# Start of a fused attention and expert kernel: first rows of three weights spread by TensorE, weights of pairs 0 and 1 prepared first, first projections in two bank pairs

## The chip, the cores and the metric

One core of one Trainium2 chip runs the whole program. The time is device microseconds of one execution. Three executions of the kernel before stand beside one profiled execution. Engines: PE is TensorE, DVE is VectorE, ACT is ScalarE, POOL is GpSimd, SP is SyncE. Each works through its own list of instructions in order, and semaphores tie the lists together.

## The reference

```python
x = states                                    # (4, 1024, 128) f32
n = layernorm(x)
q, k, v = (tanh(n @ W + b) for W, b in ((Wq, bq), (Wk, bk), (Wv, bv)))   # 16 heads of 64
a = softmax(causal(q @ k.T / sqrt(64)));  y = tanh((a @ v) @ Wo + bo)
x = x + layernorm(y)
# a second, latent attention (16 heads of 4), a router over 8 experts, top 2, 256 wide
x = x + layernorm(latent_attention_and_experts(layernorm(x)))
```

## The kernel before

The work is 4 batches of 1024 rows times 8 pairs of heads, so 32 pairs. A pair has five groups of score matmuls (`scores`), each read by an exponential on ACT (`exp`), masked at the diagonal on POOL (`mask`), summed on DVE and multiplied with the values on PE (`context`). While pair i runs, values, queries and keys of pair i + 1 are projected (`values`, `project`) and go through tanh on ACT. After the 32 pairs the latent attention and the experts follow.

Matmuls of f32 accuracy are made of f16 halves: a high part (ACT) and the remainder, the low part (DVE). The states are kept turned, with a first column of ones in place of a feature. So that this column carries the bias, the bias takes the place of row 0 of each weight, and row 0 of the weight is subtracted from every other row (`less_first`, L292). For Wv and Wq, PE spreads row 0 over the partitions by a matmul of a row of ones with it into PSUM (L331, banks 2-3 and 4-5). For Wk the row arrives spread by two broadcasting DMAs (L238). `less_first` and `weights_lo` work on all 8 pairs of heads of one weight at a time, 128x1024.

The program starts with a block of its own (L228). In it SP issues, in this order, the load of batch 0, two first rows, the spread Wk row, three bias rows, small weights, eight tiny pieces of latent biases, the other three batches and Wo (`@block.sync`). ACT issues the loads of Wv, Wq, Wk and four biases. DVE takes the moments of batch 0, normalises it and makes the weights, PE turns the batch (`turn_normal`), ACT and DVE split it (`states_hi`, `states_lo`). The block ends with a barrier of all five engines: nothing of the second block runs before the last of them, SP too, has issued its last instruction of the first.

The second block (L2397) starts on PE with `values(0)`, then `project(0, 0)` (queries) and `project(0, 1)` (keys), all three through the same two PSUM banks 4 and 5 (PJ), so that each waits for the tanh that empties them; then `scores(0, 0)`. DVE takes moments of batches 1 to 3 and normalises them meanwhile; POOL makes their deviations by two instructions (`state_deviation`, L195 and L197). PE turns batch 1 and 2 in pair 0 and batch 3 in pair 1, as each pair up to 1 has a free place in PJ. Pairs 0 to 3 are written out, then a loop follows. Within a pair PE's order is fixed by `pair` in `first_tensor`: `context(i, 3)` waits for the second mask of the pair, and the turning of the next batch stands behind it.

Of the kernel before, what the change touches and what calls it, by code (L numbers as in the profile page):

```python
# [82 lines left out]
def build(nc, states, Wq, bq, Wk, bk, Wv, bv, Wo, bo, q_w, q_b, k_w, k_b, v_w, v_b, o_w, o_b,  # L83
# [7 lines left out]
    with ExitStack() as ctx:  # L91
# [66 lines left out]
        a0 = Arena(a1.at)  # L158
        w_in = a0.take(3 * H1 * DH).rearrange("p (t n) -> p t n", t=3)
        wo_in0 = hs[:, 3 * T:3 * T + PAIRS, :]  # L160
        w_first = a0.take(3 * H1 * DH).rearrange("p (t n) -> p t n", t=3)
# [4 lines left out]
        small_in, w_got, first_got = sem("small_in"), sem("w_got"), sem("first_got")  # L166
        first_clear, w_less = sem("first_clear"), sem("w_less")
# [3 lines left out]
        SPREAD = {2: bank(2, 2), 0: bank(4, 2)}  # L171
# [55 lines left out]

        with nc.Block() as block:  # L228
            @block.sync
            def _(sp):  # L230
# [4 lines left out]
                for t, w in ((2, Wv), (0, Wq)):  # L235
                    sp.dma_start(first_rows[0:1, t, :], w[0:1, :]).then_inc(rows_got, 16)
                for rows in REST:
                    sp.dma_start(w_first[rows, 1, :], Wk[0, :].partition_broadcast(rows.stop - rows.start)  # L238
                                 ).then_inc(first_got, 16)
                for t, bias in ((2, bv), (0, bq), (1, bk)):  # L240
                    sp.dma_start(w_in[0:1, t, :], bias.rearrange("(a n) -> a n", a=1)).then_inc(first_got, 16)
# [16 lines left out]
            def _(act):  # L258
                for t, w in ((2, Wv), (0, Wq), (1, Wk)):
                    for rows in REST:  # L260
                        act.dma_start(w_in[rows, t, :], w[rows, :]).then_inc(w_got, 16)
# [3 lines left out]
                for k, (t, slot) in enumerate(((2, VSLOT), (0, QSLOT), (1, KSLOT))):  # L265
                    act.wait_ge(w_less, k + 1)
                    nc.scalar.activation(W_all[:, :, slot, :], w_in[:, t, :].rearrange("p (n c) -> p n c", n=PAIRS),
                                         ACT.Copy, scale=WSCALE).then_inc(whi_done, 1)
# [3 lines left out]
            def _(pool):  # L272
                nc.gpsimd.memset(w_first[0:1, 1, :], 0.0).then_inc(first_clear, 1)
# [17 lines left out]
            def _(dve):  # L291
                def less_first(k):  # L292
                    t = (2, 0, 1)[k]
                    if k == 0:
                        dve.wait_ge(first_clear, 1)
                        dve.wait_ge(w_got, 16 * 6)
                        dve.wait_ge(first_got, 16 * 5)
                    if t in SPREAD:
                        dve.wait_ge(first_spread, k + 1)
# [2139 lines left out]
```

## Time and profile before

| what | us |
|---|---|
| three executions | 1686.24, 1686.81, 1693.86 (median 1686.81) |
| the profiled execution | 1692.87 |
| its span | 1690.9 |
| PE busy | 1620.2 (96% of the span) |
| DVE, ACT, POOL busy | 1437.7, 1207.2, 456.0 |
| chain that ended last | PE 86%, DVE 6%, ACT 3%, issue 2%, POOL 1% |

The profile lists busy time per engine and the chain of work that ended last, followed back from the end through whatever released each step. PE is the engine of that chain nearly throughout. The start is another matter: the first two of forty slices of the span show PE 4 tenths busy and then 9 tenths.

### The profile page before, as it was taken

How to read it: one execution, taken by the hardware profiler on the slowest of the kernel's cores; microseconds unless marked ns; L12 is line 12 of the kernel's file. 1: busy time of each engine (PE TensorE's matmuls, PEld its weight loads, DVE VectorE, ACT ScalarE, POOL GpSimd, SP SyncE). 2: the span in 40 equal slices, each digit the busy share in tenths (PEclk: the TensorE clock that was granted, in tenths of full speed). 3: DMA queues.
4: the chain of work that ended last, by engine and by line, in shares of the span. 5: the costliest groups of instructions: out<-in, count | busy, mean ns of one | idle time of the engine just before them, and what ended most of it. 6: DMA issues, size and time to landing. Idle time of an engine off the chain costs nothing.

```text
span 1690.9 us, 38163 instructions
## 1 busy us (share of the span) xinstructions
PE 1620.2 (96%) x14822; PEld 713.5 (42%) x14822; DVE 1437.7 (85%) x2093; ACT 1207.2 (71%) x1205; POOL 456.0 (27%) x564
## 2 busy tenths in 40 slices
PE   4999999999999999998999999999999999989996
PEld 2444444444444444445233333333332332466774
DVE  6677778888888888897999999999999999478888
ACT  2776666666667666654887888788878888656776
POOL 2311112332322333332234232323332331220004
PEclk9999999999999999998999999999999999989998
DMA  5311101111011001011012000200030000000001
GB/s 153 71 37 38 37 20 39 38 37 37 36 37 37 34 24 38 22 32 32 14 39 49 11 13 16 48 14 13 17 73 22 14 16 14 1 1 14 13 12 50
DMA packets 46754, 53.39 MB, mean 32 GB/s; under 512 B 9309, under 2 KB 33581, under 8 KB 46638
## 3 DMA queue, kind: packets, MB, share of 16 engines
q1 hardware_dynamic: 45588, 50.06, 10.3%
q10 hardware_dynamic: 1050, 1.73, 0.4%
q8 instruction: 80, 1.31, 0.3%
q14 instruction: 36, 0.29, 0.1%
HBM read 15.59 MB, written 10.49 MB: 15 GB/s over the span
## 4 chain that ended last, share of the span: by engine, by line
PE 86%; DVE 6%; ACT 3%; issue 2%; POOL 1%; ACTq 0%; POOLq 0%; DVEq 0%
PE psum L1807 15%; PE psum L567 15%; PE psum L548 11%; PE psum L1792 9%; PE psum L1818 7%; PE psum L512 5%; PE psum L1448 5%; PE psum L1413 4%; PE psum L585 3%; DVE arena L2268 3%; PE psum L605 2%; PE psum L530 1%; ACT arena L2036 1%; PE psum L532 1%; PE psum L531 1%
## 5 line engine op out<-in xcount | busy, mean ns | idle before, releaser
L2268 DVE TENSOR_REDUCE arena<-psum 128x2 f32<-128x1024 f32 x490 | 585.6, 1220 | 39.0 <-PE psum L1818 33.0
L2036 ACT ACTIVATE arena<-psum 128x1024 f32<-128x1024 f32 x512 | 523.8, 1025 | 132.0 <-PE psum L1792 118.0
L721 ACT ACTIVATE arena<-psum 128x2048 f32<-128x2048 f32 (+1 forms) x160 | 274.0, 1712 | 231.6 <-PE psum L548 231.4
L1807 PE MATMUL psum<-arena 128*32 128x256 f32 x4096 | 327.9, 392 | 0.7
L813 POOL TENSOR_SCALAR_AFFINE_SELECT arena<-arena 128x512 f32<-128x512 f32 (+1 forms) x160 | 151.7, 966 | 521.9 <-ACT arena L721 521.9
L567 PE MATMUL psum<-arena,hs 128*64 128x512 f32 (+3 forms) x1536 | 283.0, 496 | 0.1
L548 PE MATMUL psum<-arena 64*128 64x512 f16 (+3 forms) x2304 | 216.3, 325 | 3.8 <-DVE arena L859 3.4
L1792 PE MATMUL psum<-arena 32*128 32x512 bf16 x1024 | 198.9, 385 | 3.7 <-DVE arena L2268 3.1
L1818 PE MATMUL psum<-arena 32*128 32x512 bf16 x980 | 189.1, 382 | 5.9 <-ACT arena L2036 2.4
L859 DVE TENSOR_TENSOR arena<-arena 128x1024 f16<-128x1024 f32 x64 | 80.3, 1255 | 101.0 <-ACT arena L700 101.0
L567 PEld LDWEIGHTS psum<-arena,hs 128*64 128x64 f32 x1536 | 95.9, 136 | 141.4 <-issue 125.2
L548 PEld LDWEIGHTS psum<-arena 64*128 64x128 f16 x2304 | 97.0, 94 | 136.1 <-issue 58.4
L1792 PEld LDWEIGHTS psum<-arena 32*128 32x128 bf16 x1024 | 48.2, 91 | 215.5 <-issue 145.6
L1807 PEld LDWEIGHTS psum<-arena 128*32 128x32 f32 x4096 | 81.6, 108 | 112.0 <-issue 95.1
L1519 ACT ACTIVATE arena<-psum,b1T 128x1024 f16<-128x1024 f32 x64 | 71.3, 1114 | 54.5 <-PE psum L1413 45.4
L2186 POOL TENSOR_TENSOR arena<-arena,minus_one 128x16 f32<-128x16 f32 x30 | 87.1, 2904 | 53.8 <-ACT arena L2056 53.5
L2139 POOL CAST arena<-arena 128x16 bf16<-128x16 f32 x32 | 8.1, 254 | 343.6 <-DVE arena L1208 343.6
L512 PE MATMUL psum<-arena 128*128 128x512 f16 x384 | 96.5, 389 | 3.6 <-ACT arena L700 2.0
L1448 PE MATMUL psum<-arena 128*128 128x128 f16 x1536 | 95.8, 225 | 2.2 <-DVE arena L1293 1.3
L1448 PEld LDWEIGHTS psum<-arena 128*128 128x128 f16 x1536 | 93.0, 101 | 10.1 <-issue 3.2
L1293 DVE TENSOR_TENSOR arena<-arena 128x1024 f16<-128x1024 f32 x59 | 71.9, 1222 | 25.6 <-ACT arena L1520 25.4
L1413 PE MATMUL psum<-arena 128*128 128x512 f16 x384 | 88.6, 379 | 1.7 <-ACT arena L1520 1.7
(221 smaller groups left out, 2112.7 us busy)
## 6 DMA issues: line engine op xcount, KB each, us to landing
arena<-arena SPq DMA_DIRECT2D x30, 512.0 KB, 2.9
arena<-arena SPq DMA_DIRECT2D x46, 128.0 KB, 2.2
arena<-latent_q SPq DMA_DIRECT2D x64, 64.0 KB, 2.0
arena<-latent_k SPq DMA_DIRECT2D x64, 64.0 KB, 2.0
arena<-arena SPq DMA_DIRECT2D x60, 64.0 KB, 2.4
X<-in_L_attn_states SPq DMA_DIRECT2D x4, 512.0 KB, 6.2
latent_q<-arena SPq DMA_DIRECT2D x16, 96.0 KB, 2.2
latent_k<-arena SPq DMA_DIRECT2D x16, 96.0 KB, 2.3
```

Source lines behind the costliest of these rows:

```text
L512: last = nc.tensor.matmul(PJ[:, half * HALF:(half + 1) * HALF], w_now[:, 2 * j + w, :], x_now[:, x, half * HALF:(half + 1) * HALF], start= ...
L548: last = nc.tensor.matmul(SC[:, s, c:c + w], k[rows, kt * P:(kt + 1) * P], q[rows, q0:q0 + w], start=(m == 0), stop=(m == 2), skip_group_c ...
L567: last = nc.tensor.matmul(OUT[s * DH:(s + 1) * DH, q0:q0 + w], vals[par][:, kt, s * DH:(s + 1) * DH], probs[g][:, s, c:c + w], start=first ...
L721: nc.scalar.activation(probs[g], SC[:, :, 0:WIDTH[g]], ACT.Exp, scale=DH ** -0.5).then_inc(exp_done, 1)
L813: return nc.gpsimd.affine_select(out=v, in_=v, compare_op=ALU.is_ge, fill=0.0, base=0, pattern=[[0, blocks], [1, P]], channel_multiplier=-1)
L1413: last = nc.tensor.matmul(HP[c][:, half * HALF:(half + 1) * HALF], w1_e[par][:, w, c * P:(c + 1) * P], mT[:, x, tok], start=(m == 0), stop ...
L1448: last = nc.tensor.matmul(YP[slot][:, tok], h[slot][c][:, tok], w2_e[par][:, w, c, :], start=(c == 0 and m == 0), stop=(c == FC - 1 and m ...
L1792: last = nc.tensor.matmul(dst[:, i * HALF:(i + 1) * HALF], k_rows[par][rows, kt * P:(kt + 1) * P], q_rows[par][rows, h * HALF:(h + 1) * HA ...
L1807: last = nc.tensor.matmul(OT[ROWS * c:ROWS * (c + 1), h * HALF // 2:(h + 1) * HALF // 2], v_cols[par][:, kt, 2 * pr + i, :], e_probs[u % 4 ...
L1818: last = nc.tensor.matmul(dst[:, i * HALF:(i + 1) * HALF], q_rows[par][rows, qt * P:(qt + 1) * P], k_rows[par][rows, kh * HALF:(kh + 1) * ...
L2036: nc.scalar.activation(e_probs[u % 4], src, ACT.Exp, scale=KD ** -0.5).then_inc(e_done, 1)
L2268: nc.vector.tensor_reduce(half_tops[:, kh, qt, 2 * pr:2 * pr + 2], src.rearrange("p (i c) -> p i c", i=2), AX.X, ALU.max).then_inc(top_don ...
```

## The change

Four things change.

- Row 0 of Wk is spread by PE too (bank 6-7). The three first rows are issued first on ACT's queue; the two broadcasting DMAs are gone, and the two loads of Wk's other rows move from ACT's queue to SP's. `w_in` moves to another place in SBUF, under `sums`, so the second block may still read it.
- `less_first`, `weights_hi` and `weights_lo` are cut in two parts: pairs 0 and 1 of a weight (128x256), and pairs 2 to 7 (128x768). Part 0 is done in the first block; of part 1 two subtractions are, the rest goes to the second block. SP's loads for pair 2 and DVE's first sum wait for it (`w_rest`).
- The second block starts with `project(0, 0)` into PJ and `project(0, 1)` into OUT (banks 6-7), with no wait for each other, and `values(0)` comes third. Turning and copying small biases follows it.
- Moments, deviation and normalising of batches 2 and 3 leave the start and stand inside pairs 0 and 1 on DVE and POOL. `begin_acc(0)` moves on ACT into pair 0, the ordering of latent weights into pair 1.

```diff
-        SPREAD = {2: bank(2, 2), 0: bank(4, 2)}
+        SPREAD = {2: bank(2, 2), 0: bank(4, 2), 1: bank(6, 2)}
+        SLOTS = ((2, VSLOT), (0, QSLOT), (1, KSLOT))
+        EARLY_PAIRS = (slice(0, 2), slice(2, PAIRS))
...
+        def less_first(dve, part, k):
+            t = SLOTS[k][0]
+            if part == 0:
+                dve.wait_ge(w_got[t], 16 * 3)
+                dve.wait_ge(first_spread, k + 1)
...
             @block.sync
-                for t, w in ((2, Wv), (0, Wq)):
-                    sp.dma_start(first_rows[0:1, t, :], w[0:1, :]).then_inc(rows_got, 16)
+                for t, bias in ((2, bv), (0, bq), (1, bk)):
+                    sp.dma_start(w_in[0:1, t, :], ...).then_inc(w_got[t], 16)
                 for rows in REST:
-                    sp.dma_start(w_first[rows, 1, :], Wk[0, :].partition_broadcast(rows.stop - rows.start)
+                    sp.dma_start(w_in[rows, 1, :], Wk[rows, :]).then_inc(w_got[1], 16)
...
             @block.scalar
                 for t, w in ((2, Wv), (0, Wq), (1, Wk)):
+                    act.dma_start(first_rows[0:1, t, :], w[0:1, :]).then_inc(rows_got, 16)
+                for t, w in ((2, Wv), (0, Wq)):
                     for rows in REST:
...
             @block.vector
                 state_moments(dve, 0)
-                less_first(0)
+                less_first(dve, 0, 0)
+                less_first(dve, 0, 1)
+                weights_lo(dve, 0, 0)
                 dve.wait_ge(consts, 2)
                 norm_states(dve, 0)
-                less_first(1)
-                less_first(2)
-                for k in range(3):
-                    weights_lo(k)
+                less_first(dve, 0, 2)
+                weights_lo(dve, 0, 1)
+                less_first(dve, 1, 0)
+                weights_lo(dve, 0, 2)
+                less_first(dve, 1, 1)
                 states_lo(dve, 0, bank(0, 2))
...
             def pair(i, par, last=False, norm=False):     # SP
+                if not at_least(i, 1):
+                    sp.wait_ge(w_rest, 3)
...
             def project(n, j, par):
+                if isinstance(n, int) and n == 0:
+                    if j == 1:
+                        pe.wait_ge(w_less, 6)
+                        dst = OUT
...
-            values(0, 0)
             project(0, 0, 0)
             project(0, 1, 0)
+            values(0, 0)
+            turn_biases()
             scores(0, 0, 0)
...
             def pair(i, par, last=False, norm=False):     # ACT
                 exp(i, 0)
+                (pair 0:) begin_acc(0)
...
                 mask(i, 0)                                # POOL
                 if not at_least(i, 1):
                     split_wo()
+                if not at_least(i, 2):
+                    state_deviation(pool, 2 + i)
...
                 mask(i, 3)
...
+                if not at_least(i, 2):                    # DVE, in the pair
+                    state_moments(dve, 2 + i)
                 hi_second(i, par, 0)
                 hi_second(i, par, 1)
+                if not at_least(i, 1):
+                    norm_states(dve, 2)
...
-            for b in range(1, B):
-                state_moments(dve, b)
-            dve.wait_ge(consts, 6)
-            norm_states(dve, 1)
+            less_first(dve, 1, 2)
+            weights_lo(dve, 1, 0)
+            weights_lo(dve, 1, 1)
             low_part(0, 0, 0)
-            norm_states(dve, 2)
             low_part(0, 1, 0)
-            norm_states(dve, 3)
+            state_moments(dve, 1)
+            weights_lo(dve, 1, 2)
+            norm_states(dve, 1)
```

The order of instructions shows three places. On POOL, from the start of the second block, before: three deviations, the first mask, the split of Wo (L834 to L838), and the masks of pair 0.

```order
L195 TENSOR_SCALAR rstd<-mv 128x8 [waits mv0]
L197 TENSOR_TENSOR rstd<-rstd,mhalf 128x8 [waits p0]
L195 TENSOR_SCALAR rstd<-mv 128x8 [waits mv0]
L197 TENSOR_TENSOR rstd<-rstd,mhalf 128x8 [waits p0]
L195 TENSOR_SCALAR rstd<-mv 128x8 [waits mv0]
L197 TENSOR_TENSOR rstd<-rstd,mhalf 128x8 [waits p0]
L813 AFFINE_SELECT arena<-arena 128x4x128 [waits exp_done]
L813 AFFINE_SELECT arena<-arena 128x2x128
L834 TENSOR_SCALAR hs<-hs 128x1024 [waits wo_got]
L836 CAST arena<-hs 128x8x128 [waits wo_split]
L838 TENSOR_TENSOR arena<-hs,arena 128x8x128 [waits wo_split]
L813 AFFINE_SELECT arena<-arena 128x4x128 [waits exp_done]
```

And the same stretch of POOL now:

```order
L197 TENSOR_SCALAR rstd<-mv 128x8 [waits mv0]
L199 TENSOR_TENSOR rstd<-rstd,mhalf 128x8 [waits p0]
L854 AFFINE_SELECT arena<-arena 128x4x128 [waits exp_done]
L854 AFFINE_SELECT arena<-arena 128x2x128
L875 TENSOR_SCALAR hs<-hs 128x1024 [waits wo_got]
L877 CAST arena<-hs 128x8x128 [waits wo_split]
L879 TENSOR_TENSOR arena<-hs,arena 128x8x128 [waits wo_split]
L197 TENSOR_SCALAR rstd<-mv 128x8 [waits mv0]
L199 TENSOR_TENSOR rstd<-rstd,mhalf 128x8 [waits p0]
L854 AFFINE_SELECT arena<-arena 128x4x128 [waits exp_done]
```

The deviation of batch 2 (a wait for `mv0`) now stands between the split of Wo and the second mask of pair 0.

On DVE inside pair 0, from the low part of the next pair's keys to the low half of the turned batch 1, before (L859 is the low part, L924 a sum, L226 the turned batch):

```order
L859 TENSOR_TENSOR arena<-arena 128x1024 [waits tanh_done]
L924 TENSOR_TENSOR arena<-arena 128x2x512 [waits sum_hi,exp_done]
L924 TENSOR_TENSOR arena<-arena 128x2x512 [waits sum_hi]
L226 TENSOR_TENSOR arena<-psum,arena 128x1024 [waits xt_hi]
L932 TENSOR_TENSOR arena<-arena 128x2x512 [waits sum_hi,masked]
```

And now:

```order
L901 TENSOR_TENSOR arena<-arena 128x1024 [waits tanh_done]
L187 BN_STATS stats<-X 128x6 [waits x_in2]
L187 BN_STATS stats<-X 128x6 x7
L190 BN_AGGR mv<-stats 128x2 [waits d0]
L190 BN_AGGR mv<-stats 128x2 x7
L968 TENSOR_TENSOR arena<-arena 128x2x512 [waits sum_hi,exp_done]
L968 TENSOR_TENSOR arena<-arena 128x2x512 [waits sum_hi]
L209 TENSOR_SCALAR acc<-X,mv,rstd 128x127 [waits rstd0]
L209 TENSOR_SCALAR acc<-X,mv,rstd 128x127 x7
L228 TENSOR_TENSOR arena<-psum,arena 128x1024 [waits xt_hi]
```

Sixteen instructions of statistics and eight of normalising have come in between.

On ACT the second block begins, before (L706 is the tanh of the values, L697 and L700 the two of queries or keys, L721 the first exponential):

```order
L791 COPY b1T<-psum 128x16
L792 COPY b_lat<-psum 128x1
L784 ACTIVATE acc<-bo_b 128x1024
L796 COPY w_lat<-w_lat_in 128x64 x2
L706 ACTIVATE hs<-psum 128x1024 [waits vproj_done]
L697 ACTIVATE arena<-psum 128x1024 [waits qk_done]
L700 ACTIVATE arena<-psum 128x1024
L697 ACTIVATE arena<-psum 128x1024 [waits qk_done]
L700 ACTIVATE arena<-psum 128x1024
L721 ACTIVATE arena<-psum 128x2048 [waits scores_done]
```

And now:

```order
L247 ACTIVATE arena<-arena 128x6x128 [waits w_less] x2
L726 ACTIVATE arena<-psum 128x1024 [waits qk_done]
L729 ACTIVATE arena<-psum 128x1024
L726 ACTIVATE arena<-psum 128x1024 [waits qk_done]
L729 ACTIVATE arena<-psum 128x1024
L735 ACTIVATE hs<-psum 128x1024 [waits vproj_done]
L247 ACTIVATE arena<-arena 128x6x128 [waits w_less]
L826 COPY b1T<-psum 128x16 [waits biasT_ps]
L827 COPY b_lat<-psum 128x1
L750 ACTIVATE arena<-psum 128x2048 [waits scores_done]
L817 ACTIVATE acc<-bo_b 128x1024
```

Two weight copies stand ahead of the tanhs of the queries, and the tanh of the values and a third weight copy stand behind those of the keys.

## Rows read from the trace of the kernel before

**Rows 1.** Windows: stretch, length, busy of each engine (instructions), PE clock, DMA.

```profile
500.00:700.00 200.00, 199.01 (x1685) 91.90 (x1682) 170.37 (x231) 133.34 (x116) 64.78 (x74) 1.00 0.10 36
```

**Rows 2.** Timeline of SP's queue, 0 to 26 us: start, duration, issue.

```profile
4.81 8.98 SPq L246 DMA_DIRECT2D w_lat_in<-in_L_ffn_k_w  x1
13.84 0.43 SPq L246 DMA_DIRECT2D w_lv<-in_L_ffn_v_w  x1
...
23.29 1.58 SPq L255 DMA_DIRECT2D hs<-in_L_attn_Wo  x1
25.27 1.39 SPq L460 DMA_DIRECT2D arena<-arena  x1
```

**Rows 3.** DMA from 10 to 11 us: packets, MB, share; q10 is ACT's.

```profile
q10 hardware_dynamic: 63, 0.21, 86.7%
q1 hardware_dynamic: 62, 0.02, 14.4%
```

**Rows 4.** The same from 13 to 14 us; q1 is SP's.

```profile
q1 hardware_dynamic: 1229, 0.02, 76.0%
```

**Rows 5.** Timeline of the first block: start, duration, instructions, idle before.

```profile
8.19 7.16 PE L331 MATMUL psum<-arena 1*128 1x512 f32 x8 [8.19 <-DMA arena<-in_L_attn_Wq]
...
18.01 1.94 PE L215 MATMUL psum<-ident,hs 128*128 128x128 f32 x8 [2.66 <-DVE hs L207]
...
21.12 0.99 ACT L221 CAST arena<-psum 128x1024 f16<-128x1024 f32 x1
...
23.44 1.23 DVE L226 TENSOR_TENSOR arena<-psum,arena 128x1024 f16<-128x1024 f32 x1
```

**Rows 6.** The chain that ended last, 25 to 56 us: start, duration, work.

```profile
29.15 2.76 PE psum L512 x6
...
36.70 1.02 ACT arena L697
...
38.78 1.24 DVE arena L859
40.06 2.76 PE psum L548 x18
...
54.19 1.43 PE psum L548 x18
```

**Rows 7.** Timeline, 25 to 38 us: what moves to another place.

```profile
25.40 1.07 ACT L784 ACTIVATE acc<-bo_b 128x1024 f32<-128x1024 f32 x1
...
26.36 0.51 ACT L796 COPY w_lat<-w_lat_in 128x64 f32<-128x64 f32 x2
...
29.75 1.61 DVE L185 BATCH_NORM_STATS2 stats<-X 128x6 f32<-128x128 f32 x8
...
31.40 0.64 DVE L188 BATCH_NORM_AGGREGATE mv<-stats 128x2 f32<-128x6 f32 x8
...
32.13 0.24 POOL L195 TENSOR_SCALAR rstd<-mv 128x8 f32<-128x8 f32 x1 [0.22 <-DVE mv L188]
32.46 1.67 POOL L197 TENSOR_TENSOR rstd<-rstd,mhalf 128x8 f32<-128x8 f32 x1
...
35.15 2.13 DVE L207 TENSOR_SCALAR acc<-X,mv,rstd 128x127 f32<-128x127 f32 x8
```

**Rows 8.** Timelines of DVE, POOL and PE in pair 0.

```profile
54.82 1.22 DVE L859 TENSOR_TENSOR arena<-arena 128x1024 f16<-128x1024 f32 x1 [0.40 <-ACT arena L700]
...
57.69 1.61 POOL L813 TENSOR_SCALAR_AFFINE_SELECT arena<-arena 128x512 f32<-128x512 f32 x2 [5.50 <-ACT arena L721]
...
59.35 1.94 PE L567 MATMUL psum<-arena,hs 128*64 128x512 f32 x12
```

**Rows 9.** The same three in pair 1.

```profile
76.69 1.23 DVE L859 TENSOR_TENSOR arena<-arena 128x1024 f16<-128x1024 f32 x1 [2.48 <-ACT arena L700]
...
79.56 1.61 POOL L813 TENSOR_SCALAR_AFFINE_SELECT arena<-arena 128x512 f32<-128x512 f32 x2 [12.31 <-ACT arena L721]
...
81.67 1.94 PE L567 MATMUL psum<-arena,hs 128*64 128x512 f32 x12
```

More of the change, by code:

```diff
@@ L157, in build @@
         ones = a1.take(DH)
-        a0 = Arena(a1.at)
+        SUMS_AT = a1.at + 18 * S
+        a0 = Arena(SUMS_AT, ARENA - S)
         w_in = a0.take(3 * H1 * DH).rearrange("p (t n) -> p t n", t=3)
         wo_in0 = hs[:, 3 * T:3 * T + PAIRS, :]
-        w_first = a0.take(3 * H1 * DH).rearrange("p (t n) -> p t n", t=3)
         x_in = [sem(f"x_in{b}") for b in range(B)]
         wo_got, wo_split = sem("wo_got"), sem("wo_split")
-        small_in, w_got, first_got = sem("small_in"), sem("w_got"), sem("first_got")
-        first_clear, w_less = sem("first_clear"), sem("w_less")
+        small_in, w_got = sem("small_in"), [sem(f"w_got{t}") for t in range(3)]
+        w_less, w_rest = sem("w_less"), sem("w_rest")
         first_rows = a0.take(3 * H1 * DH).rearrange("p (t n) -> p t n", t=3)
@@ L259, in _ @@
                 for t, w in ((2, Wv), (0, Wq), (1, Wk)):
+                    act.dma_start(first_rows[0:1, t, :], w[0:1, :]).then_inc(rows_got, 16)
+                for t, w in ((2, Wv), (0, Wq)):
                     for rows in REST:
-                        act.dma_start(w_in[rows, t, :], w[rows, :]).then_inc(w_got, 16)
+                        act.dma_start(w_in[rows, t, :], w[rows, :]).then_inc(w_got[t], 16)
                 for dst, src in ((bo_b, bo), (vb_b, v_b), (ob_b, o_b), (rb_b, router_b)):
                     act.dma_start(dst[:, :], src.partition_broadcast(P)).then_inc(small_in, 16)
[L265 to L268, printed above, removed]
+                for k in range(3):
+                    weights_hi(act, 0, k)
                 states_hi(act, 0, bank(0, 2))
@@ L511, in project @@
                     for m, (w, x) in enumerate(passes):
-                        last = nc.tensor.matmul(PJ[:, half * HALF:(half + 1) * HALF], w_now[:, 2 * j + w, :],
+                        last = nc.tensor.matmul(dst[:, half * HALF:(half + 1) * HALF], w_now[:, 2 * j + w, :],
                                                 x_now[:, x, half * HALF:(half + 1) * HALF], start=(m == 0), stop=(m == 2))
@@ L525, in values @@
                 elif n > 0:
-                    pe.wait_ge(tanh_done, 4 * n)
+                    pe.wait_ge(vals_ready, n)
+                else:
+                    pe.wait_ge(tanh_done, 2)
                 for t in range(T):
@@ L740, in pair @@
                     copy_out(i - 1, 1 - par)
+                else:
+                    begin_acc(0)
                 if last:
@@ L766, in pair @@
                     take_states(2 + i)
+                if isinstance(i, int) and i == 1:
+                    order_latent_weights()
             def first_states():
@@ L983, in pair @@
                     invert(i - 1)
+                    if not at_least(i, 2):
+                        norm_states(dve, 3)
                 else:
```

94 lines of the change are left out of this document (52 added, 42 removed).

## The prediction, made before the changed kernel ran

> **What bounds the kernel now.** I read the busy shares, then windows, then the timelines of the first 90 us engine by engine, SP's queue among them, and the chain of waits for the same stretch. In the middle PE is busy 199.0 of 200 us [rows 1]: the change touches nothing there, and time won or lost before the loop is carried to the end whole, since no engine idles later that could absorb it. So the question is only when PE reaches pair 2. Up to there three stages follow each other: the first block to its barrier, the new start up to the first scores, and pairs 0 and 1.
>
> **The barrier.** Which wait ends last there? DVE's last instruction ends at 23.44 + 1.23 = 24.67 [rows 5]. SP's last issue ends at 23.29 + 1.58 = 24.87, and its first of the second block stands at 25.27 [rows 2]. They nearly tie, so speeding DVE alone gains 0. DVE will be early. Its new end, step by step: PE spreads three rows instead of two, 7.16 x 3/2 = 10.7 us [rows 5]. The rows no longer queue behind batch 0; in the trace they were there at 8.19 [rows 5]. Three issues of 0.43 [rows 2] from the start of the block (0.8) end at 2.1, so the rows come between 2.1 and 8.2; I take 4, the lower part, as they are the first of their queue. The Trainium skill ("DMA: Bandwidth & Descriptors", its table of the fixed cost) gives about 2.0 us fixed per transfer, an estimate of about 4 for the third of three issues; no row shows a transfer of this size alone. PE is then done at 14.8, turns the batch in 1.94 (16.9), ACT copies in 0.99 (18.0), DVE makes the low half in 1.23: 19.3 [rows 5]. With the rows at 8.2 it is 23.5. DVE's other work is shorter (a quarter or three quarters of each 128x1024 step) and fits into those waits.
>
> SP is the other limit. Its issue of k_w stands 8.98 us and ends at 13.79; from there the rest of its list takes 24.87 - 13.79 = 11.1 us, and none of it changes [rows 2]. What holds k_w is that the small pieces of q_w ahead of it do not drain: from 10 to 11 us SP's queue moves 62 packets beside 63 of ACT's, which carry 0.21 MB, and from 13 to 14, with ACT's weights gone, 1229 [rows 3, 4]. So it ends about 1.5 us after the weights have landed. The change takes 127 rows of 4 KB (0.52 MB) out of them, at 0.23 MB per us [rows 3] 2.2 us; ACT starts its weights three issues (1.3 us) later, of which I charge 0.7, because batch 0 fills the engines meanwhile. The barrier comes 1.5 us earlier, bounds 0 (the drain is not shortened) and 5.4 (SP not the limit at all; DVE is, at 19.3). The first PE instruction moves from 25.3 to 23.8.
>
> **From the barrier to the first scores.** Before, 14.75 us lie from 25.3 to the scores at 40.06 [rows 6]: values, tanh, queries, two tanhs, keys, two tanhs, low part. Now queries and keys run back to back, 2 x 2.76 = 5.5 us [rows 6]. `project(0, 1)` waits for six subtractions, the last of 128x768, about 0.95 us on DVE: covered by the 2.76 of the queries. ACT's two weight copies (0.8 us each, three quarters of the 1.07 of a 128x1024 copy [rows 7]) are done before the queries are. Behind the keys the path is the old one: from ACT's first tanh of keys at 36.70 to the scores at 40.06 are 3.36 us. So scores start 8.9 us after the barrier instead of 14.75: 5.85 us less. Values (24 matmuls of 128 columns, as many columns as the queries' six of 512, so up to 2.76) and the two small turnings of biases fit beside the 3.36 us of tanh and low part; if they don't, they cost what stands over, under 1 us.
>
> The first scores took 2.76 us where the same 18 instructions later take 1.43 [rows 6]: TensorE at 1.2 and then 2.4 GHz. Before, PE had idled 3.4 us ahead of them. Now it works for some 8 us almost without a pause, and pauses for about 1. I count the 1.33 us as won. The other bound is 0. A row speaks for that bound: the spreading matmuls held PE busy 7.16 us and the turning behind them was still slow (1.94 us for 8) [rows 5], but there only one row of the array was used. The Trainium skill ("TensorE: Matmul & The Clock Gate", Part 1) has the clock throttled by default and released by sustained activity; by it the scores run at 2.4 GHz, by the row of the spreading they would not, and the sum would be 1.3 us longer. Start to first exponential: 5.85 + 1.33 = 7.2 us less. Together with the barrier the first exponential is 8.7 us early.
>
> **What pairs 0 and 1 give back.** The moved statistics cost nothing as DVE's time, since DVE has gaps, but they are on a chain: POOL's second mask now stands behind a deviation, that behind moments, these behind DVE's low part of the next keys. Pair 0, in times of the trace: the low part ends at 56.04 [rows 8]. `begin_acc(0)`, 1.07 us [rows 7], now stands between ACT's first exponential and the tanh of values; it costs between 0 and 1.07 here, by the gaps of ACT and PE around it, and I take 0.4: 56.45. Moments 1.61 + 0.64 [rows 7]: 58.75. Deviation 0.24 + 1.67 and the handing over [rows 7]: 60.8. Mask 1.61: 62.4. PE's `context(0, 3)` stood at 59.35 [rows 8]: 3.05 us late, nothing else to do behind it, as the turning is next in line. Normalising (2.13) stands before the low half of batch 1 and so delays that of batch 2, for which `values(2)` waits: 0.35 more. 3.4 in all. Pair 1: low part ends at 77.92, plus 2.25, 2.05 and 1.61 is 83.8, against 81.67 [rows 9]: 2.15. Here normalising batch 3 is on the chain to its turning and to `values(3)`: 1.25, and the ordering of latent weights (0.51 [rows 7]) stands before ACT's next exponential: 3.9 in all. The wait on `w_rest` is met before the first mask; DVE reaches its first sum 2.1 us late (moments and normalising of batch 1, 4.4 us, now stand behind the low parts), which the gap before the next low part takes up. Bounds for both pairs together: 0 (the chains hidden) and 9.2 (7.3 plus 1.9, if a low part is lengthened by POOL beside it).
>
> **Sum.** -1.5 - 7.2 + 3.4 + 3.9 = -1.4 us on the profiled execution: 1692.87 becomes 1691.5. That execution is 6.1 us above the median of the runs, near the slowest of the three; carried over to the median: 1685.4.
>
> **The rivals.**
> - *The barrier falls to DVE.* k_w's stall is shorter than I think, and SP ends at or before 19.4. For it: packets alternate one for one, so any shift in when ACT's bulk ends counts fully. Against: the 11.1 us of issues behind k_w would have to start at 8.3, before the weights have landed. 3.9 us more: 1681.5.
> - *The masks are not late.* The statistics run in gaps and pairs 0 and 1 take as long as before: gain 8.7 less 1, so 1679. Against it stands the order on POOL, which can't pass the deviation. A barrier at DVE's end besides would make 1675.
> - *Slower: the moved statistics cost more than the start gains.* Place: POOL's second mask in pairs 0 and 1. Price 9.2 against 5.85, with the barrier at 24.9 and the scores at 1.2 GHz: +3.4, so 1690.2. It decides from the point where the two pairs lose more than the first exponential is early. For it: each piece has a bound in the rows; against: all three must come together.
> - *The change doesn't do what it says:* the rows arrive at 8.2 and PE's third spreading sets the end of the block, 23.5 + 0.4, about where SP puts it anyway: 1685.5, not to be told from the forecast by time.
>
> **How the numbers follow.** The forecast, with the last rival, 0.58; barrier at DVE or between, 0.17; masks not late, 0.10; slower, 0.15. A measurement of this kernel tells about 0.5%, 8.4 us, from no change. The forecast, the first rival and most of the slower one lie within it; the masks' rival with an early barrier passes it, and of the slower case only a piece with still worse pairs. The three runs before lie 7.6 us apart, which widens the tails a little. Faster 0.11, same 0.83, slower 0.06. The range for 8 in 10 leaves out the deepest of the masks' rival and the end of the slower one: 1679.5 to 1691.5.
>
> **What would show it.** Right: PE's first matmul at about 23.8 with SP's Wo issue ending just before it, DVE done near 19.3, k_w's stall to about 12.3; scores of pair 0 about 8.9 us behind that matmul and 1.43 long; POOL's second mask in pairs 0 and 1 ending two to three us late, PE idle before `context(0, 3)` and `context(1, 3)`. Wrong: SP's stall still ending at 13.8, DVE ending after 22, or PE without idle time in pairs 0 and 1.

## The result and the profile after

| kernel | executions | median us | lowest to highest |
|---|---|---|---|
| before | 20 | 1692.87 | 1684.73 to 1697.21 |
| changed | 20 | 1697.37 | 1689.61 to 1700.07 |

The changed kernel is slower: ratio 1.0032, 95% interval 1.0019 to 1.0045, so 3.2 to 7.6 us. Forecast were 1.4 us less. Of the three times shown before the prediction two lay low; over twenty executions the median of the kernel before is 6 us higher, and only the ratio tells about the change. The changed kernel's profiled execution took 1689.61 us, less than the 1692.87 of the one before, though it has lost time by pair 3. Why that can be stands in the last section.

A point that every trace has is PE's start on the projection of the queries of pair 3. It comes at 90.29 us before and at 93.08 now. From there to the last output matmul of the pairs both traces need 689 us, within 0.1. So the loss of these 2.8 us is made in the first 93 us.

The start first. SP's queue of the changed kernel (start, duration, issue) answers to [rows 2]:

```profile
3.94 7.05 SPq L275 DMA_DIRECT2D w_lat_in<-in_L_ffn_k_w  x1
11.04 0.43 SPq L275 DMA_DIRECT2D w_lv<-in_L_ffn_v_w  x1
...
20.27 1.57 SPq L284 DMA_DIRECT2D hs<-in_L_attn_Wo  x1
```

The stall ends at 10.99, not 13.79, and SP still issues last, at 21.84. The instructions of the other engines that answer to [rows 5] and [rows 6], from the timeline (start, duration, instructions, idle before):

```profile
5.62 10.57 PE L344 MATMUL psum<-arena 1*128 1x512 f32 x12 [5.62 <-DMA arena<-in_L_attn_Wk]
...
19.17 1.23 DVE L228 TENSOR_TENSOR arena<-psum,arena 128x1024 f16<-128x1024 f32 x1
...
22.29 5.28 PE L528 MATMUL psum<-arena 128*128 128x512 f16 x12 [4.20 <-PEq L260]
...
30.97 1.48 PE L566 MATMUL psum<-arena 64*128 64x512 f16 x18 [1.03 <-DVE arena L901]
...
32.49 1.88 ACT L750 ACTIVATE arena<-psum 128x2048 f32<-128x2048 f32 x1 [1.18 <-PE psum L566]
```

DVE is done at 20.4, PE starts the second block at 22.29 (25.31 before), the scores come 8.7 us later and take 1.48 us, and the first exponential starts at 32.49 instead of 42.85: 10.4 us early. Now pair 0 on DVE, POOL and PE, against [rows 8]:

```profile
35.89 3.96 DVE L209 TENSOR_SCALAR acc<-X,mv,rstd 128x127 f32<-128x127 f32 x8 [1.90 <-POOL rstd L199]
...
46.22 1.21 DVE L901 TENSOR_TENSOR arena<-arena 128x1024 f16<-128x1024 f32 x1
47.36 1.63 DVE L187 BATCH_NORM_STATS2 stats<-X 128x6 f32<-128x128 f32 x8
49.03 0.64 DVE L190 BATCH_NORM_AGGREGATE mv<-stats 128x2 f32<-128x6 f32 x8
49.59 2.45 DVE L968 TENSOR_TENSOR arena<-arena 128x1024 f32<-128x1024 f32 x2
...
49.76 1.12 POOL L197 TENSOR_SCALAR rstd<-mv 128x8 f32<-128x8 f32 x1 [6.01 <-DVE mv L190]
50.97 2.60 POOL L199 TENSOR_TENSOR rstd<-rstd,mhalf 128x8 f32<-128x8 f32 x1
53.54 1.58 POOL L854 TENSOR_SCALAR_AFFINE_SELECT arena<-arena 128x512 f32<-128x512 f32 x3
...
48.53 0.83 PE L566 MATMUL psum<-arena 64*128 64x256 f16 x12
54.59 3.68 PE L585 MATMUL psum<-arena,hs 128*64 128x512 f32 x12 [5.23 <-POOL arena L854]
58.20 1.46 PE L217 MATMUL psum<-ident,acc 128*128 128x128 f32 x8
```

Read it from PE upward. PE has nothing to do for 5.23 us, because POOL's second mask starts only at 53.54; POOL has idled 6.01 us for the moments and then takes 3.8 us for a deviation that took 2.0 in [rows 7]. After the gap the same matmuls take 3.68 us instead of 1.94. The windows of the changed kernel (stretch, length, busy of PE, PEld, DVE, ACT and POOL, granted clock, DMA) show why:

```profile
47.00:49.00 2.00, 2.00 (x22) 1.29 (x20) 1.99 (x9) 0.99 (x2) 0.00 (x0) 1.00 0.72 80
...
52.00:54.50 2.50, 0.00 (x0) 0.00 (x0) 0.94 (x3) 0.00 (x0) 2.50 (x4) 0.53 0.71 129
54.50:58.30 3.80, 3.71 (x13) 1.35 (x14) 3.80 (x9) 0.00 (x0) 0.62 (x2) 0.50 0.69 84
...
60.00:65.00 5.00, 4.97 (x60) 2.89 (x56) 3.00 (x6) 5.00 (x5) 0.99 (x2) 1.00 0.51 119
```

The last number but two of a window is the granted clock: 1.00 is 2.4 GHz, 0.50 is 1.2 GHz. It falls while PE idles, and stays at 1.2 GHz for the next 5 us of PE's work. Pair 1 repeats it, against [rows 9]:

```profile
77.58 1.12 POOL L197 TENSOR_SCALAR rstd<-mv 128x8 f32<-128x8 f32 x1 [12.99 <-DVE mv L190]
78.78 2.61 POOL L199 TENSOR_TENSOR rstd<-rstd,mhalf 128x8 f32<-128x8 f32 x1
81.37 1.58 POOL L854 TENSOR_SCALAR_AFFINE_SELECT arena<-arena 128x512 f32<-128x512 f32 x3
...
82.42 3.26 PE L585 MATMUL psum<-arena,hs 128*64 128x512 f32 x12 [3.34 <-POOL arena L854]
```

### The profile page after: what moved, and what is told of

Read it like the earlier page. It is cut to its first block, busy times and chain, and to the rows that moved or that the text cites. A ratio compares the mean times of both kernels' runs of the same rounds, so it can differ in the third digit from the quotient of the medians.

```text
span 1687.8 us, 38180 instructions
## 1 busy us (share of the span) xinstructions
PE 1617.6 (96%) x14826; PEld 710.0 (42%) x14826; DVE 1440.4 (85%) x2099; ACT 1207.1 (72%) x1208; POOL 457.8 (27%) x563
## 4 chain that ended last, share of the span: by engine, by line
PE 84%; DVE 8%; ACT 3%; issue 3%; POOL 1%; ACTq 0%; POOLq 0%; DVEq 0%
PE psum L1857 15%; PE psum L585 15%; PE psum L566 11%; PE psum L1842 9%; PE psum L1868 7%; PE psum L528 5%; PE psum L1498 5%; PE psum L1463 4%; PE psum L603 3%; DVE arena L2318 3%; PE psum L623 2%; PE psum L548 1%; ACT arena L2086 1%; PE psum L1897 1%; PE psum L549 1%
```

## The experiments

All are read at the same points: PE's first matmul of the second block, the first exponential, PE's projection of the queries of pair 2 and of pair 3. "Pair 0" is from the first exponential to the queries of pair 2, "pair 1" from those to the queries of pair 3.

| kernel | second block | first exp | pair 0 | pair 1 | queries of pair 3 |
|---|---|---|---|---|---|
| before | 25.31 | 42.85 | 25.1 | 22.3 | 90.29 |
| changed | 22.29 | 32.49 | 32.8 | 27.8 | 93.08 |
| deviation behind mask | 22.98 | 32.74 | 33.0 | 27.4 | 93.13 |
| PE filled | 23.14 | 32.61 | 31.9 | 26.7 | 91.24 |
| before, statistics moved | 24.66 | 38.38 | 30.7 | 27.4 | 96.44 |
| before, projections alone | 24.37 | 40.27 | 25.1 | 22.3 | 87.72 |
| changed, statistics in front | 22.28 | 40.78 | 26.0 | 22.7 | 89.47 |
| changed, q_w last | 20.20 | 29.68 | 33.3 | 27.8 | 90.74 |
| statistics spread | 22.47 | 32.48 | 26.6 | 22.7 | 81.77 |
| statistics spread, q_w last | 21.12 | 31.15 | 26.6 | 22.7 | 80.45 |
| before again | 24.96 | 42.49 | 25.5 | 22.3 | 90.26 |
| changed again | 23.26 | 33.35 | 32.4 | 27.8 | 93.53 |
| batch 2 ahead | 23.10 | 33.30 | 28.1 | 26.7 | 88.09 |
| no weights' part | 24.84 | 34.31 | 26.6 | 22.3 | 83.27 |

**The deviation behind the mask.**

```diff
                 mask(i, 0)
-                if not at_least(i, 2):
-                    state_deviation(pool, 2 + i)
                 mask(i, 3)
+                if not at_least(i, 2):
+                    state_deviation(pool, 2 + i)
                 mask(i, 4)
```

> The changed kernel, with one edit: on POOL the deviation of batches 2 and 3 stands behind the second mask of pairs 0 and 1, not ahead of it. Theory (the deviation ahead of the mask holds PE's context(i, 3)): PE's idle time before context(0, 3), 5.2 us in the changed kernel, falls under 1 us, and the matmuls of it take 1.9 us again, not 3.7, as the clock stays at 2.4 GHz; a shorter wait appears before the turning of batch 2, some 2 to 3 us, since normalising still waits for the deviation. PE's second score group of pair 2, at 91.25 us in the changed kernel, comes 3 to 5 us earlier. Rival (DVE's added work delays the pairs, wherever POOL's deviation stands): it comes within 1 us of 91.25.

Half of it came. `context(0, 3)` is on time and takes 1.94 us, but the second wait is 6 us instead of 2 to 3, and the sum is the same, 93.13. PE's timeline of this kernel:

```profile
49.53 1.94 PE L585 MATMUL psum<-arena,hs 128*64 128x512 f32 x12
57.46 1.97 PE L217 MATMUL psum<-ident,acc 128*128 128x128 f32 x8 [5.98 <-DVE arena L228]
59.36 2.44 PE L566 MATMUL psum<-arena 64*128 64x512 f16 x18
```

The gap ends with L228 on DVE, the low half of batch 1, which DVE does after it has normalised batch 2, for which it waits for POOL's deviation. The theory as I put it, that POOL's mask is held, names only one of two chains through the same deviation; DVE's order holds PE as long. By its number the rival was right (the second score group of pair 2 stands at 91.64, against 91.25), but not by its reason: DVE's added work is cheap elsewhere, as the spread statistics show below.

**PE filled.**

```diff
                 scores(i, 4, par)
+                if isinstance(i, int) and i < 2:
+                    pe.wait_ge(exp_done, 5 * i + 5)
+                    for _ in range((13, 9)[i]):
+                        nc.tensor.matmul(bank(1)[:, 0:HALF], W_all[:, 0, 0, :], xT_all[:, 0, 0, 0:HALF], ...)
                 context(i, 3, par)
```

> The changed kernel, and in pairs 0 and 1 PE does 13 and 9 more matmuls of 512 columns into a free half of the score banks (their result is never read), once the last exponential of the pair is done and before context(i, 3). They add no wait: PE idles there anyway. It separates the wait from what the clock costs behind it. Theory: the idle gap before context(0, 3) is still there but only about 2 us long at a time, the clock stays at 2.4 GHz, context(0, 3) takes 1.9 instead of 3.7 us, context(1, 3) 1.9 instead of 3.3, the turnings 1.1 instead of 1.4: 3.5 us of the loss are the clock's, and the second score group of pair 2 comes at 87.7. Rival (the long durations come from something else, such as SBUF traffic of POOL and DVE beside them): durations and 91.25 stay.

```profile
51.69 2.98 PE L656 MATMUL psum<-arena 128*128 128x512 f16 x13 [2.21 <-ACT arena L755]
54.72 1.94 PE L585 MATMUL psum<-arena,hs 128*64 128x512 f32 x12
57.80 1.09 PE L217 MATMUL psum<-ident,acc 128*128 128x128 f32 x8 [1.13 <-DVE arena L228]
```

The clock stays up: 1.94 and 1.09 us again. So the long durations are the clock's, and not POOL's or DVE's traffic. But the gain at pair 3's queries is 1.84 us, not 3.5 (by the length of the two pairs 2.0 us against the first trace of the changed kernel and 1.5 against the second): the turning, no longer late by PE, now waits 1.13 us for DVE's L228. Half of what the clock costs hides a wait behind it.

**The statistics alone, in the kernel before.**

```diff
+                    state_deviation(pool, 2 + i)      # POOL, pairs 0 and 1, ahead of mask(i, 3)
...
+                    state_moments(dve, 2 + i)         # DVE, pairs 0 and 1, behind low_part(i + 1, 1)
+                    norm_states(dve, 2)               # pair 0; batch 3 in pair 1
...
-            for b in range(1, B):
-                state_moments(dve, b)
+            state_moments(dve, 1)
...
-            norm_states(dve, 2)
             low_part(0, 1, 0)
-            norm_states(dve, 3)
```

> The kernel before, with only the statistics of batches 2 and 3 (moments, deviation, normalising) moved into pairs 0 and 1, as the change has them. In the kernel before, the first exponential starts at 42.85 and the second score group of pair 2 at 88.52, 45.67 us later; in the changed kernel 58.76 us lie between. Theory (moved statistics are what gives the start's gain back): most of the 13 us appear here alone: 8 to 11 us more between the two, somewhat less than in the changed kernel because batch 1's moments and normalising stay ahead of the first scores, and the first exponential is no more than 1 us earlier. Rival (the give-back comes from the new start, such as the third part of the weights, which DVE and ACT still have to do): under 3 us more.

Pairs 0 and 1 take 58.1 us, 10.6 more than before: the moved statistics alone bring most of the 13.1. What I had wrong is the first exponential: 38.38, 4.5 us earlier, not 1. Of these, 0.7 are an earlier barrier, and the other 3.8 are not DVE's work but TensorE's clock. PE's queries, keys and first scores in the kernel before:

```profile
29.15 2.74 PE L512 MATMUL psum<-arena 128*128 128x512 f16 x6 [1.12 <-ACT hs L706]
...
33.92 2.74 PE L512 MATMUL psum<-arena 128*128 128x512 f16 x6 [2.03 <-ACT arena L700]
...
40.06 2.74 PE L548 MATMUL psum<-arena 64*128 64x512 f16 x18 [3.40 <-DVE arena L859]
```

And in this run:

```profile
28.50 1.47 PE L512 MATMUL psum<-arena 128*128 128x512 f16 x6 [1.12 <-ACT hs L706]
...
32.00 1.47 PE L512 MATMUL psum<-arena 128*128 128x512 f16 x6 [2.03 <-ACT arena L700]
...
36.87 1.48 PE L548 MATMUL psum<-arena 64*128 64x512 f16 x18 [3.40 <-DVE arena L860]
```

PE waits 1.12, 2.03 and 3.40 us in both, so the statistics did not hold it; the three groups of matmuls run at 2.4 GHz here and at 1.2 before. These levels are read from the durations, as the profile puts the granted clock at 1.00 for this stretch in both traces. Why the clock was up in this one is open: the second trace of the kernel before has 2.74 us three times, like the first.

**The order of projections alone, in the kernel before.**

```diff
-            values(0, 0)
             project(0, 0, 0)
             project(0, 1, 0)      # into banks 6 and 7
+            values(0, 0)
```

> The kernel before, with only the order of the first projections changed: queries, keys (into banks 6 and 7), values, and the tanhs in that order. Theory: PE no longer waits for tanh, but DVE becomes the limit: moments of three batches, two normalisings and two low parts stand ahead of the first scores, 25.3 + 6.6 + 2.1 + 1.2 + 2.1 + 1.2 = 38.5, so the scores start at 38.6 to 39.0 instead of 40.06, and 1.3 us more come from the clock if PE stays at 2.4 GHz: first exponential at 40 to 41.5. The rest of pairs 0 and 1 as before. Rival (the order on PE is what limits the start): scores at 25.3 + 8.9 = 34.2.

The first exponential is at 40.27, in the range, pairs 0 and 1 are unchanged, and 2.6 us are won in all, of which 0.9 is an earlier barrier. The scores:

```profile
37.49 2.74 PE L555 MATMUL psum<-arena 64*128 64x512 f16 x18 [6.86 <-DVE arena L867]
```

DVE is the limit, as the theory had it, and the rival's 34.2 is far off. The clock did not stay up: the scores take 2.74 us (granted clock 0.50), so the exponential is in the range only because the scores start early. From the barrier to the first exponential it is 15.9 us here, 17.5 in the kernel before and 10.2 in the changed one. So the order of the projections limits the old start; with that order changed, the statistics ahead of the low parts do; and only both together free it.

**Statistics back in front, in the changed kernel.**

```diff
+            for b in range(1, B):
+                state_moments(dve, b)
+            norm_states(dve, 1)
             low_part(0, 0, 0)
+            norm_states(dve, 2)
             low_part(0, 1, 0)
+            norm_states(dve, 3)
```

> The changed kernel, with the statistics of batches 1 to 3 back ahead of the pairs, in the order of the kernel before (and the last third of the weights behind them). Theory: pairs 0 and 1 take what they took before, about 46 us from the first exponential (45.67 before, 58.76 in the changed kernel) to the second score group of pair 2, but the start's gain shrinks, because DVE now stands before the low parts: moments of three batches end at about 31.6, the first low part at 35, the second at 38.4, first exponential at about 40. The group at 86, 2.5 us ahead of the kernel before. Rival (the loss in the pairs comes from the split weights or the new banks): over 52 us between the two.

48.7 us for the two pairs against 47.4 before and 60.6 changed: the split weights and the new banks cost the pairs 1.3 us at most. The first exponential is at 40.78, about as expected; with the 1.3 us, queries of pair 3 come 0.8 us ahead of before, not 2.5.

**q_w last.**

```diff
-                for dst, src in ((w_lat_in[:, 0:LAT], q_w.rearrange(...)[:, :, 0:KD]),
-                                 (w_lat_in[:, LAT:], k_w), ...
+                for dst, src in ((w_lat_in[:, LAT:], k_w), ...
...
                 sp.dma_start(wo_in0, Wo...)
+                sp.dma_start(w_lat_in[:, 0:LAT], q_w.rearrange(...)[:, :, 0:KD])
```

> The changed kernel, with SP issuing the load of q_w (2048 pieces of 16 bytes) last instead of ahead of k_w. Theory (SP's stall behind q_w sets the barrier, 7.05 us in the changed kernel): the stall is gone, SP's last issue ends before 18, and the barrier falls to DVE, whose last instruction ended at 20.4: PE's first projection at 20.7 to 20.9 instead of 22.29, and all that follows 1.4 to 1.6 us earlier. Rival (DVE and SP are limited by the same transfers, or the loads of the other batches, now earlier, take the weights' bandwidth): no change, or later than 22.3.

SP's issues of this kernel:

```profile
3.24 0.39 SPq L274 DMA_DIRECT2D w_lat_in<-in_L_ffn_k_w  x1
...
15.72 1.75 SPq L284 DMA_DIRECT2D w_lat_in<-in_L_ffn_q_w  x1
```

The issue of k_w takes 0.39 us. SP is done at 17.5, DVE at 19.9, and the second block starts at 20.20: 2.1 to 3.1 us earlier than in the two traces of the changed kernel, where 1.4 to 1.6 were expected. DVE is done 0.5 us sooner than in the changed kernel's first trace; the rest may be how traces differ, as those with one first block lie up to 1 us apart there. The gain stands at pair 3's queries, 2.3 to 2.8 us.

**Statistics spread.**

```diff
+            state_deviation(pool, 2 + i)      # POOL: right behind mask(i, 0), ahead of split_wo
...
                 lo_second(i, par)             # DVE, pair 1 only
+                    state_moments(dve, 3)
                 low_part(i + 1, 0, 1 - par)
                 hi_first(i, par)
+                    norm_states(dve, 3)
...
+            state_moments(dve, 1)
             low_part(0, 0, 0)
             low_part(0, 1, 0)
-            state_moments(dve, 1)
+            state_moments(dve, 2)
             weights_lo(dve, 1, 2)
             norm_states(dve, 1)
```

> The changed kernel, with the statistics where their engines have time and nobody waits. DVE: moments of batch 1 before the first low part, of batch 2 after the second, of batch 3 in pair 1 ahead of the low part of queries, normalising of batch 3 ahead of the low part of keys. POOL: deviation of batches 2 and 3 right behind the first mask of pairs 0 and 1 and ahead of the split of Wo. Theory: the start stays (first exponential at 32.5), PE waits less than 1 us before context(0, 3) and context(1, 3), pairs 0 and 1 take 47 us, the second score group of pair 2 comes at about 80, 8 us ahead of the kernel before, and the time falls by about 8 us under it (0.5%) and 11 to 12 under the changed kernel. Rival (DVE's added work in the pairs costs as much wherever it stands): 55 us or more for the pairs.

```profile
35.59 0.24 POOL L197 TENSOR_SCALAR rstd<-mv 128x8 f32<-128x8 f32 x1
35.91 1.67 POOL L199 TENSOR_TENSOR rstd<-rstd,mhalf 128x8 f32<-128x8 f32 x1
...
49.55 1.94 PE L585 MATMUL psum<-arena,hs 128*64 128x512 f32 x12 [0.20 <-POOL arena L854]
52.29 1.09 PE L217 MATMUL psum<-ident,acc 128*128 128x128 f32 x8 [0.80 <-DVE arena L228]
...
72.73 1.94 PE L585 MATMUL psum<-arena,hs 128*64 128x512 f32 x12
```

The same instructions on the same engines, in other places, cost 1.9 us instead of 13.1. PE waits 0.20 and 0.80 us in pair 0 and not at all in pair 1. Queries of pair 3 come at 81.77, 8.5 us ahead of before. The time follows, but with less certainty: ratio to before 0.9971, interval 0.9949 to 0.9993, so 1 to 9 us (10 executions, median 1685.28, against 1687.02 in 19 of the kernel before beside them).

**Statistics spread, q_w last:** both edits together.

> The kernel of the run before it in this call (statistics spread), and q_w loaded last. Theory: both gains add: PE's first projection at 20.8, second score group of pair 2 at about 78.5, the time 9 to 10 us under the kernel before. Rival: the barrier's gain is lost again to a wait in pair 0, since the order of DVE there leaves no slack: no difference from the run before it.

The gains add: the second block starts 1.35 us earlier than in the run above, and pair 3's queries come 1.3 us earlier. Ratio 0.9960, interval 0.9940 to 0.9979 (median 1683.92), so 3.5 to 10 us faster than before, where 9 to 10 were expected. It has the lowest ratio of these kernels, though its interval overlaps with those of the other two that were timed ten times. Against the changed kernel it was not timed directly; the two ratios make it about 12 us faster, and the queries of pair 3 12.6.

**Both kernels again,** without an edit.

> The kernel before, unchanged, profiled once more. Theory (the barrier of the shown trace, 25.31, is a late one; two kernels with the same first block had it at 24.4 and 24.6): first matmul of the second block at 24.3 to 25.3, and projection of pair 3's queries (90.29 in the shown trace) 64.98 us after it within 0.3, so that it comes at 89.3 to 90.3. Rival (the stretch behind the barrier varies as much): other than 64.7 to 65.3 us behind it.

> The changed kernel, unchanged, profiled once more. Theory: first matmul at 22.3 to 23.1, projection of pair 3's queries (93.08) 70.8 us behind it within 0.5, at 93.1 to 93.9: against the kernel before the loss at this point is 3.5 to 4 us rather than the 2.8 of the first pair of traces. The time is in one of the two groups of its 20 executions (1690 or 1697.5), and the trace shows which stretch of half clock it has: near 780 to 800, near 1440 to 1470, or neither. Rival (the groups differ in something at the start): a time near 1697 with no such stretch.

Before: 24.96, and 65.30 us from there to pair 3's queries, 0.3 more than expected. Changed: 23.26, then 70.27, 0.5 less. At pair 3's queries the two differ by 3.3 us here and by 2.8 in the first traces; I had expected 3.5 to 4 now. The changed kernel's time, 1699.46, goes with a stretch of half clock behind the pairs, and that of the kernel before, 1687.41, with none (last section). Over all traces with the same first block, the second starts at 24.8 on average with the old one (five) and at 22.8 with the new one (seven): the barrier has come 2.0 us earlier.

**Batch 2 ahead.**

```diff
             state_moments(dve, 1)
+            state_moments(dve, 2)
             weights_lo(dve, 1, 2)
...
                 mask(i, 0)
+                state_deviation(pool, 2 + i)      # moments of batch 3 still behind low_part(2, 1)
```

> The changed kernel, with the moments of batch 2 ahead of the pairs (behind those of batch 1) and both deviations behind the first mask; moments of batch 3 stay in pair 1 behind the low part of keys, and are needed by a deviation which now stands ahead of all later masks of that pair. Theory (a deviation on POOL must not stand where its moments come late): pair 0 is cured, first exponential to projection of pair 2's queries falls from 32.8 us to about 27, pair 1 still costs what it costs in the changed kernel, 27.8 us instead of 22.4 (from pair 2's to pair 3's projection), so pair 3's at about 87. Rival (both pairs suffer from one common thing, such as DVE falling behind): neither is cured.

Pair 0 falls from 32.8 to 28.1 (27 expected), pair 1 stays high, 26.7, and PE waits before its `context(1, 3)`:

```profile
78.50 1.94 PE L585 MATMUL psum<-arena,hs 128*64 128x512 f32 x12 [3.34 <-POOL arena L854]
```

Curing pair 0 does not cure pair 1, so it isn't one common thing such as DVE falling behind. And behind the same 3.34 us of idle time that brought the clock down in the changed kernel's pair 1 (3.26 us for these matmuls), it stays at 2.4 GHz here (1.94 us, granted clock 1.00): that is the 1.1 us between the two kernels' pairs 1.

**No weights' part:** the projections of the fourth experiment and the spread statistics, in the kernel before.

> The kernel before, with its first block as it was (no third spread row, no split of the weights), but with the first projections in two bank pairs and the statistics spread as in the fastest kernel so far. It tells what the weights' part of the change is worth. Theory (it only moves the barrier, by some 2 us, since the rest of the start is the order of projections and DVE's list): second block at 24.4 to 25.3, first exponential 10.0 us later, projection of pair 3's queries at 83.7 to 84.9, 2 to 3 us behind the kernel with the weights' part (81.77), 5 to 6 ahead of the kernel before. Rival (preparing pairs 0 and 1 first is what lets the new start work): first exponential later than 37.

First exponential at 34.31, 9.5 us behind the barrier, queries of pair 3 at 83.27, just ahead of the range expected: 7 us ahead of before, 1.5 behind the spread kernel with the weights' part. Ratio to before 0.9968, interval 0.9945 to 0.9991. Preparing pairs 0 and 1 first is not what frees the start; with the third spread row it moves the barrier, and that is 1.5 to 2 us in the traces. The two ratios, 0.9968 and 0.9971, are too uncertain to show it.

## Why the prediction was wrong

**The barrier was right in mechanism and near in size.** SP's stall behind q_w set it and still does; forecast 1.5 us earlier, 2.0 on average over the traces (3.0 in the pair shown: there the trace before is 0.5 later than its average and the changed one 0.5 earlier). DVE's end was forecast at 19.3 and is 20.4. PE's rows came at 5.6 and not 4; the steps of the forecast add up to 18.9 from 4, not to 19.3, and to 20.5 from 5.6.

**From the barrier to the first exponential** I forecast 7.2 us less, and 7.3 came: 17.5 before, 10.2 now. The scores take 1.48 us, so they run at 2.4 GHz, as I chose against the row of the spreading matmuls [rows 5]. What I held to be the reason for the slow scores before, 3.4 us of idle time, is not enough of one: with the same 3.40 us ahead of them they take 1.48 in "before, statistics moved". There the old start is 3.8 us shorter by the clock alone, so the 7.3 hold against a start that ran at 1.2 GHz, as in both traces of the kernel before.

**What pairs 0 and 1 give back is the step that failed:** 7.3 us forecast with an upper bound of 9.2, 13.1 measured. The places and the order of waits were right, the sizes not. For pair 0, 7.7 us instead of 3.4:
- The moments end 1.3 us later behind the first exponential than I had (17.2 instead of 15.9). I wrote that the gap before the next low part takes up DVE's delay. It didn't: DVE reaches its first sum 4.2 us late, not 2.1, mostly because normalising batch 1 took 3.96 us beside POOL's mask and split of Wo, not 2.13. The last of these sums took 2.24 us (0.43 before), so the low part of the queries was already late.
- The deviation takes 3.8 us, not 2.05: it now starts beside two sums of DVE, in [rows 7] it didn't. Together with the first, `context(0, 3)` comes 5.6 us late instead of 3.05, offset in part by a shorter mask.
- The gap is then long enough for the clock to fall, 2.1 us on the two next steps. I had weighed the clock for the scores at the start and not at the one place where I had put a new wait on PE. The filled run shows that this is the clock, and that about half of it would be paid as a wait otherwise. Whether it falls is not settled by the length of the gap alone: in pair 1 it fell behind 3.34 us here and didn't in "batch 2 ahead".

For pair 1, 5.4 instead of 3.9: `context(1, 3)` 3.4 us late instead of 2.15, 1.6 us of half clock, and 0.4 behind it. My upper bound counted POOL and DVE beside each other once, for a low part, and the clock not at all.

**The sum,** by traces: -3.0 - 7.3 + 13.1 = +2.8 in the first pair, +3.3 in the second. The ratio says +5.4 us with an interval from 3.2. The executions lie in a lower and an upper group (last section). Between the lower groups the medians differ by 3.5 us (1686.5 and 1690.0), between the upper ones by 3.8 (1694.0 and 1697.8), which fits the traces. The rest is that 4 of 20 executions of the changed kernel lie in the lower group, and 8 of 20 of the kernel before. In later sets of the kernel before it was 10 of 19 and 5 of 13, so this share moves without any change; whether the change moves it too is not shown.

**The level.** 1697.37 stands 12.0 us above the 1685.4 of the forecast. Of these, 6.1 are that the three executions shown lay low for their kernel, 1.4 the gain that didn't come, and 4.5 the loss by the two medians. The range up to 1691.5 left out even the median of the kernel before, 1692.87.

**The rivals.** "The moved statistics cost more than the start gains" is what happened, at the place named, with 0.15. I priced it by 9.2 against a start without the faster scores, and said that three things must come together. The start was as good as forecast; a larger price alone did it. The range ended at 1691.5 because of that same bound. The chance for a change within 0.5% holds.

## What to carry to other kernels

A step moved to an engine with idle time is free only if nobody stands behind it in that engine's order: here two instructions on POOL and twenty-four on DVE per pair stood ahead of what PE waited for next, and the same instructions at earlier places, where PE had nothing to wait for behind them, gave back 11 of 13 us. A new wait on PE can cost more than its length: in pair 0 an idle time of 5.2 us brought the clock down in all three traces that have it, and that cost 1.7 to 2.6 us on the next two steps; in pair 1 about 3.3 us cost 1.6 to 1.7 in four traces of five, and nothing in the fifth. So work the sum out with and without it. And price a moved step beside what runs at its new place, not by its duration at the old one.

## What the runs showed of the hardware

**Two groups of times.** The executions of both kernels lie in groups some 7 us apart (before: 8 of 20 from 1684.7 to 1688.8, 12 from 1692.4 up; changed: 4 from 1689.6 to 1690.1, 14 from 1696.3 up, and two between). The traces show stretches of half clock after the pairs, which some executions have and others don't. PE from the last output of the pairs to the first f32 score product of the next stage takes 16.0 to 16.5 us in ten of the fourteen traces, and 21.3 to 23.5 in the other four (the first of before, the second of the changed kernel, statistics in front, q_w last). The stage behind takes 675.4 to 676.8 us in ten, and 684.2 in four (filled, projections alone, both spread kernels). In the spread kernel the granted clock is 0.50 from 1445 to 1460 us, with PE busy throughout. The windows of the kernel before (busy of PE, PEld, DVE, ACT, POOL; granted clock; DMA) show the first:

```profile
785.00:790.00 5.00, 5.00 (x21) 2.01 (x22) 2.29 (x9) 2.66 (x3) 1.31 (x6) 0.50 0.57 116
790.00:795.00 5.00, 5.00 (x23) 3.39 (x23) 2.62 (x8) 1.02 (x1) 0.00 (x0) 0.50 0.29 67
```

and those of the changed kernel's first trace the same place at full clock:

```profile
785.00:790.00 5.00, 4.90 (x37) 2.25 (x36) 3.87 (x14) 3.75 (x5) 0.73 (x3) 1.00 0.52 139
790.00:795.00 5.00, 4.40 (x37) 3.36 (x38) 3.56 (x11) 1.42 (x2) 0.58 (x3) 1.00 0.59 120
```

This is why the changed kernel's shown execution is the shorter one: it is 2.8 us behind at pair 3 and gains 5.3 at this place; the stages behind add up to the other 0.6 of 3.1. One trace of a kernel can't tell a difference of a few us by its span; a common point early in it can. Why an execution meets such a stretch is not explained here, and no run tried to prevent it.

**POOL and DVE beside each other.** The deviation's two instructions take 0.24 and 1.67 us with no sum of DVE beside them, and 1.12 and 2.60 with two. The eight normalising instructions take 2.13 us alone and 3.96 beside POOL's mask and split of Wo. The Trainium skill ("SBUF — State Buffer", Who interferes with whom) has a DVE instruction with two SBUF inputs and a GpSimd instruction that reads SBUF exclude each other; the sums have two SBUF inputs, and the trace agrees in direction there, 0.9 us longer on each. It doesn't everywhere: in the spread kernel a sum of 128x768 (0.95 us) lies within the deviation's second instruction, and that takes 1.67 us all the same. Of normalising, it has the two-port modes of `tensor_scalar` in contention too; no run here tells those apart.

**A small transfer can hold a queue.** The load of q_w, 2048 pieces of 16 bytes and 32 KB in all, held SP's next issue, that of k_w, for 7 to 9 us in twelve traces; with q_w issued last, k_w's issue took 0.39 us in both traces.
